# Self-attention row maxima: two key halves in two row halves of the array, one 1024-column reduction

## The reference, cut to what matters

```
q, k, v = (h @ wq), (h @ wk), (h @ wv)            # 1024 x 1024, as 16 heads of 64
sim  = einsum("bhid,bhjd->bhij", q, k) * 64**-0.5 # 1024 x 1024 for each head
attn = softmax(sim)                               # over the keys j
out  = einsum("bhij,bhjd->bhid", attn, v)
```

## Time and profile before

| | |
|---|---|
| median of 3 runs | 2324.59 us (2319.39 to 2327.59) |
| the profiled execution's own time | 2328.06 us |
| its span, first to last instruction | 2326.3 us |
| TensorE busy | 2142.8 us (92%) |
| VectorE busy | 1743.6 us (75%) |
| ScalarE busy | 1476.1 us (63%) |
| GpSimd busy | 1155.2 us (50%) |
| self-attention's maxima on TensorE (L831) | 1024 matmuls, 390.5 us busy |
| their reductions on VectorE (L1411) | 1024, 680.2 us busy |

### The profile page before, as it was taken

One profiled execution on the slowest core, in us unless ns is written; L12 is line 12 of the kernel. 1 busy time (PEld: TensorE's weight loads), 2 busy tenths in 40 slices (PEclk: granted clock), 3 DMA queues, 4 the chain that ended last, 5 costly groups with the idle time before them and its releaser, 6 DMA issues.

```text
span 2326.3 us, 59157 instructions
## 1 busy us (share of the span) xinstructions
PE 2142.8 (92%) x25392; PEld 1434.0 (62%) x25392; DVE 1743.6 (75%) x3148; ACT 1476.1 (63%) x1948; POOL 1155.2 (50%) x730
## 2 busy tenths in 40 slices
PE   4999999999899999989989999998998999999899
PEld 1566666675556666667556666666755666667675
DVE  5888888557588888755768888866576888886664
ACT  2788788345388888823547887773353888786342
POOL 3666665233076766622326766652223667664231
PEclk8999999999999999999999999999999999999999
DMA  3222221000132222001032222100103223210000
GB/s 107 71 73 52 61 62 38 10 31 23 51 105 52 58 74 63 18 10 38 24 83 73 52 75 77 43 27 1 38 23 81 70 61 83 61 36 20 10 11 19
DMA packets 60165, 114.19 MB, mean 49 GB/s; under 512 B 9344, under 2 KB 21632, under 8 KB 59904
## 3 DMA queue, kind: packets, MB, share of 16 engines
q1 hardware_dynamic: 59904, 110.41, 17.5%
HBM read 55.72 MB, written 4.19 MB: 26 GB/s over the span
## 4 chain that ended last, share of the span: by engine, by line
PE 65%; DVE 21%; ACT 9%; issue 3%; DMA 1%; POOL 1%; SPq 0%; POOLq 0%; DVEq 0%; ACTq 0%
PE scores L861 7%; DVE minima L1411 7%; PE scores L854 7%; PE work L831 7%; PE scores L746 6%; PE scores L748 6%; PE scores L747 6%; DVE prob L1426 4%; PE work L746 4%; PE work L747 4%; PE work L748 4%; PE work L883 3%; PE work L879 3%; PE work L881 3%; ACT prob L1214 3%
## 5 line engine op out<-in xcount | busy, mean ns | idle before, releaser
L693 POOL TENSOR_TENSOR prob<-prob 128x1024 f16<-128x1024 f32 x256 | 584.7, 2284 | 556.0 <-ACT prob L1215 545.2
L1411 DVE TENSOR_REDUCE minima<-work 128x1 f32<-128x512 f32 x1024 | 680.2, 684 | 43.0 <-PE work L831 29.4
L1214 ACT ACTIVATE prob<-scores 128x1024 f32<-128x1024 f32 x512 | 525.6, 1026 | 129.2 <-PE scores L861 112.0
L1215 ACT ACTIVATE prob<-scores 128x1024 f16<-128x1024 f32 x512 | 523.3, 1022 | 0.0
L883 PE MATMUL work<-vals,prob 128*128 128x65 f16 x4096 | 429.6, 196 | 0.0
L881 PE MATMUL work<-vals,prob 128*128 128x64 f16 x4096 | 429.4, 193 | 0.0
L879 PE MATMUL work<-vals,prob 128*128 128x65 f16 x4096 | 429.0, 193 | 0.4
L879 PEld LDWEIGHTS work<-vals,prob 128*128 128x128 f16 x4096 | 383.1, 99 | 62.1 <-issue 3.1
L881 PEld LDWEIGHTS work<-vals,prob 128*128 128x128 f16 x4096 | 379.9, 97 | 58.2
L831 PE MATMUL work<-ka,qa 128*128 128x512 f16 x1024 | 390.5, 386 | 24.0 <-DVE minima L1411 18.2
L883 PEld LDWEIGHTS work<-vals,prob 128*128 128x128 f16 x4096 | 380.3, 97 | 0.0
(11 more groups left out here) (160 smaller groups left out, 4179.0 us busy)
## 6 DMA issues: line engine op xcount, KB each, us to landing
qa<-staged_q SPq DMA_DIRECT2D x128, 128.0 KB, 2.3
ka<-staged_k SPq DMA_DIRECT2D x128, 128.0 KB, 2.3
raw_even<-in_pairs SPq DMA_DIRECT2D x32, 384.0 KB, 3.3
raw_odd<-in_pairs SPq DMA_DIRECT2D x32, 384.0 KB, 3.3
raw_odd<-in_pieces SPq DMA_DIRECT2D x20, 512.0 KB, 3.7
raw_even<-in_pieces SPq DMA_DIRECT2D x20, 512.0 KB, 3.6
qb<-staged_q SPq DMA_DIRECT2D x64, 128.0 KB, 2.3
kb<-staged_k SPq DMA_DIRECT2D x64, 128.0 KB, 2.3
```

The source lines that it names most:

```text
L693: pool.tensor_tensor(prob[1][:, slot, :], prob32[:, slot, :], prob[0][:, slot, :], ALU.subtract).then_inc(a.polished, 1)
L1214: act.activation(prob32[:, n % RING, :], source, ACT.Exp)
L1215: act.activation(prob[0][:, n % RING, :], source, ACT.Exp)\
L1411: dve.tensor_reduce(minima[:, t, h:h + 1], out[:, :], AX.X, ALU.max, negate=True)\
```

## The change

Only the upper parts are multiplied for the maxima (q_up·k_up), so a product needs 64 rows. The two key halves of a tile are issued one after the other, the first on the head's own 64 rows (`qa` and `ka`), the second on the other 64 rows, where `qa` already holds the upper query parts and a new buffer `kx` holds the upper key parts of keys 512 to 1023. They write the two halves of one tensor `peaks` of two banks, and one reduction of 1024 columns writes the tile's column of `shift16` itself. `combine` and `shift_combined` go. The step stands whole before the score. There is one `peaks` buffer (`PEAK_RING` 1), which the shift's transpose uses too. `kx` lies in `t32` and is filled by one more DMA for each head (`MOVES` 14 in place of 12).

```diff
-SCORE_RING, PEAK_RING, HIGH_RING = 2, 2, 1
-MOVES = 12
+SCORE_RING, PEAK_RING, HIGH_RING = 2, 1, 1
+MOVES = 14
 def maxima(par, head):
-    tiles = [[Step("max", (t, h), par, head, 0) for h in range(BLKS)] for t in range(TILES)]
+    tiles = [[Step("max", t, par, head, 0)] for t in range(TILES)]
     tiles[0] = first + tiles[0]
-    tiles[-1] = tiles[-1] + [Step("combine", 0, par, head, 0)]
 def self_unit(pair, head):
-        out += [step for step in peaks_of[s] if step.kind == "arrive"] + peaks[:1]
+        out += peaks_of[s]
         out += placed[s]
         out.append(Step("score", s, par, head, 0))
         out += [take(step) for step in placed[s] if step.kind in HIGH]
-        out += peaks[1:] + [step for step in peaks_of[s] if step.kind == "combine"]
 # buffers
-        work = [ps(f"work{i}", BLK) for i in range(4)]
-        self_peaks = [work[0], work[2]]
+        peaks = ps("peaks", 2 * BLK)
+        work = [peaks[:, 0:BLK], ps("work1", BLK), peaks[:, BLK:2 * BLK], ps("work3", BLK)]
+        kx = [t32[:, i, :, :].rearrange("p c n -> p (c n)").bitcast(F16)[:, 0:BLK] for i in range(2)]
 # SP
-                            moves = [(ka_[mine, :], up), (ka_[others, :], low), (kb_[mine, :], up)]
+                            moves = [(ka_[mine, :], up), (ka_[others, :], low), (kb_[mine, :], up),
+                                     (kx[step.par][others, :], up[:, BLK:TOKENS])]
 # TensorE
-                    pe.wait_ge(a.peak_free, pace.n(*PEAK) + 1)
+                    pe.wait_ge(a.peak_free, pace.n(*PEAK) + PEAK_RING)
-                        pe.matmul(out[:, :], qa[par][head][:, t * P:(t + 1) * P],
-                                  ka[par][head][:, h * BLK:(h + 1) * BLK], start=True, stop=True)\
-                            .then_inc(a.peak_full, 1)
+                        mine, others = [slice(r, r + DH) for r in (head * DH, (1 - head) * DH)]
+                        for h, (rows_, keys) in enumerate(((mine, ka[par][head][mine, 0:BLK]),
+                                                           (others, kx[par][others, :]))):
+                            last = pe.matmul(work[2 * h], qa[par][head][rows_, s * P:(s + 1) * P], keys,
+                                             start=True, stop=True)
+                        last.then_inc(a.peak_full, 1)
                     elif step.kind == "shift":
-                        pe.wait_ge(a.shift_combined, pace.n("shift") + 1)
 # VectorE
-                        dve.tensor_reduce(minima[:, t, h:h + 1], out[:, :], AX.X, ALU.max, negate=True)\
+                        dve.tensor_reduce(shift16[:, s:s + 1], peaks[:, :], AX.X, ALU.max, negate=True)\
                            .then_inc(a.peak_free, 1)
-                    elif step.kind == "combine":
-                        dve.wait_ge(a.peak_free, pace.n(*PEAK) + PEAK_RING)
-                        dve.tensor_reduce(shift16[:, :], minima[:, :, :], AX.X, ALU.min)\
-                           .then_inc(a.shift_combined, 1)
```

More of the change, by code:

```diff
@@ L215, in self_unit @@
     for s in range(TILES):
-        peaks = [step for step in peaks_of[s] if step.kind == "max"]
         if s == TILES - 1 and after:
             out.append(Step("shift", 0, *nxt, 0))
-        out += [step for step in peaks_of[s] if step.kind == "arrive"] + peaks[:1]
+        out += peaks_of[s]
         out += placed[s]
@@ L390, in build @@
         prob = [sb(f"prob{i}", [P, 4, TOKENS], F16) for i in range(2)]
-        minima = sb("minima", [P, TILES, 2])
         shift16 = sb("shift16", [P, TILES], F16)
@@ L445, in build @@
         names = ("peak_full peak_free work_full work_high work_free scores_full exp_done refined polished probs_used "
-                 "outs_free inverse_ready head0_ready head1_ready shift_combined row_ready")
+                 "outs_free inverse_ready head0_ready head1_ready row_ready")
         a = collections.namedtuple("Sems", names)(*[sem(f"self_{n}") for n in names.split()])
@@ L766, in next_peak @@
                 def next_peak():
-                    pe.wait_ge(a.peak_free, pace.n(*PEAK) + 1)
-                    return self_peaks[pace.here(*PEAK) % PEAK_RING]
+                    pe.wait_ge(a.peak_free, pace.n(*PEAK) + PEAK_RING)
                 def weight(kind, c, column):
@@ L825, in do @@
                     elif step.kind == "max":
-                        if head == 1 and s == (0, 0):
+                        if head == 1 and s == 0:
                             pe.wait_ge(a.head1_ready, pace.n("arrive", times=8 * MOVES) + CREDIT)
-                        out = next_peak()
-                        t, h = s
-                        pe.matmul(out[:, :], qa[par][head][:, t * P:(t + 1) * P],
-                                  ka[par][head][:, h * BLK:(h + 1) * BLK], start=True, stop=True)\
-                            .then_inc(a.peak_full, 1)
+                        next_peak()
+                        mine, others = [slice(r, r + DH) for r in (head * DH, (1 - head) * DH)]
[4 more added lines that the diff above has]
+                        last.then_inc(a.peak_full, 1)
                     elif step.kind == "shift":
-                        out = next_peak()
-                        pe.wait_ge(a.shift_combined, pace.n("shift") + 1)
-                        pe.transpose(out[0:TILES, 0:P // 2].bitcast(F16), shift16[:, :], ident16[:, :])\
+                        next_peak()
+                        pe.transpose(work[0][0:TILES, 0:P // 2].bitcast(F16), shift16[:, :], ident16[:, :])\
                           .then_inc(a.peak_full, 1)
@@ L1405, in do @@
                     elif step.kind == "max":
[L1406 to L1410, removed]
-                        dve.tensor_reduce(minima[:, t, h:h + 1], out[:, :], AX.X, ALU.max, negate=True)\
+                        next_peak()
+                        dve.tensor_reduce(shift16[:, s:s + 1], peaks[:, :], AX.X, ALU.max, negate=True)\
                            .then_inc(a.peak_free, 1)
-                    elif step.kind == "combine":
-                        dve.wait_ge(a.peak_free, pace.n(*PEAK) + PEAK_RING)
-                        dve.tensor_reduce(shift16[:, :], minima[:, :, :], AX.X, ALU.min)\
-                           .then_inc(a.shift_combined, 1)
                     elif step.kind == "shift":
-                        out = next_peak()
+                        next_peak()
                         dve.wait_ge(a.row_ready, pace.n("shift", times=16) + CREDIT)
-                        dve.tensor_copy(shift_rows[:, :], out[0:TILES, 0:P // 2].bitcast(F16))\
+                        dve.tensor_copy(shift_rows[:, :], work[0][0:TILES, 0:P // 2].bitcast(F16))\
                            .then_inc(a.peak_free, 1)
```

## The result

The changed kernel takes 2356.21 us (median of 4, 2352.65 to 2358.05), the kernel before 2325.03 (4, 2319.39 to 2327.59): 1.0136 times as long, 95% interval 1.0113 to 1.0158. It is slower by 31 us, where 15 were forecast. The sign was right, but by luck: only half of the size was forecast, the term that was to make the kernel slower is not there, and the loss comes mostly from places that the sum had at nothing or too small.

A forecast was written before the change was run, and what follows sets the result against it. TensorE's stream was taken to bound most of a unit, VectorE's order its end. 64 × (0.52 − 0.34) = +11.5 us, and +4 before the units, gave +15 us: 2340 us, 0.6% slower, range 2238 to 2388.

The forecast's parts named there:

- The sign: Whole kernel: slower, by 15 us; chances 0.44 slower, 0.43 faster, 0.13 no change.
- What bounds the kernel: In a unit: TensorE back to back for most of it, VectorE's order deciding at its end.
- TensorE, the cost after: Six pairs of 64-row products a unit: 0.495 us each with 0.235 excess, 2.89 against 2.37, +0.52 us a unit.
- rivals 1 and 2: Rival 1: 64 rows come and go free, 2250 us, chance 0.30; rival 2: products not side by side, about 2406, 0.12.
- VectorE at the unit's end: Chain at the unit's end: reduction and `combine` leave, a wait for the copy enters; −0.34 us a unit, bounds 0 and −0.6.
- Before the units: Tiles standing alone, one buffer: 2.6 us more in the first round, with the later rounds +4 us together.
- DMAs: SP's queue, two more DMAs for each pair of heads: costs nothing; up to 19 us if the cover went.
- Rival 3: Bare steps: one buffer makes TensorE wait 0.3 us in 3 of 8 steps; 58 us, 2398 us, chance 0.10.

The follow-up runs named there:

- the serial rows: The changed kernel with both products of a tile on the head's own 64 rows, one after the other, without the two added DMAs: 2434.54 us.
- The longer queue alone: The kernel before with the change's two more DMAs for each pair of heads, into a buffer that nothing reads: 2336.09 us.
- full rows: The changed kernel with both products of a tile over all 128 rows and without the two added DMAs: 2368.52 us.
- the early split: The changed kernel with GpSimd's split of weights in pair 0 at step 0 of the unit instead of step 3: 2344.31 us.
- The order alone: The kernel before with both products of a tile ahead of the score in steps 0 to 6, two banks and `combine` kept: 2318.22 us.
- three edits: The later fetch, the early split and the later gather together: 2312.94 us in the changed kernel, 2319.31 us in the kernel before.
- the later fetch: The changed kernel with the weight fetch of step 6 moved behind the shift row in SP's queue: 2346.75 us.
- the later gather: The changed kernel with VectorE's gather of step 6 moved from ahead of the shift's copy to behind it: 2337.25 us.
- the order and all three: The kernel before with both products of a tile ahead of the score, plus the three edits: 2307.09 us.

## Why the prediction was right or wrong

- **What bounds the kernel**: right. The two places, TensorE's stream and VectorE's order at the unit's end, are where the steady units moved.
- **TensorE, the cost after**: the step that failed first, mis-sized. The mechanism (side by side, and a drain) was right, and rivals 1 and 2 are refuted by the rows of the pair and by the serial rows. But 0.495 was 0.41: beyond one product it is 0.195 in all, where 0.031 + 0.235 + 0.015 was taken., the eight transposes, were carried over almost whole, and a pair of 64 rows comes in and out for less. 6 × 0.41 − 0.085 = 2.38 against 2.37: the term of +0.52 a unit, 33 us of the sum, is zero; a pair of units takes 45.54, not 45.9. The forecast's sign hung on it, so that the right sign is luck.
- **VectorE at the unit's end**: the wait that turns into a wait for the copy came as told, and the end itself is 0.4 shorter (0.34 forecast). But "out" for the reduction of tile 6 overlooked the take that now stands behind a whole reduction: L746 waits 8.7 us for L1382 (4.1 before). An undisturbed unit is 0.23 longer or 0.26 shorter, about nothing on the mean, where −0.34, or 22 us of the sum, was taken. It is the upper bound that the prediction named for the term. So the two largest terms, +33 and −22 us, were both near nothing: −2.1 us for all undisturbed units.
- **Before the units**: too small. +2.6 was +6.0. The alternation with one buffer is dearer at the lower clock (4.4 in place of 2.6), and the first product comes 2.6 later. Of that, 1.7 us is there at the first query DMA already (33.29 against 31.60). It belongs mostly to this execution: in the four other traces of the changed kernel in which this start is unaltered the DMA is issued at 31.77 to 32.37. The added move ahead of the first pair, 0.64, was left out of the sum.
- **DMAs**: wrong, and the step that failed plainly. "So nothing" rested on one pair in which the shift row left at 170.39 with 0.6 of room. Other pairs had none: six scores waited for the row before the change already. The longer queue alone, with the unit's end as before, makes the odd units 5.5 us longer, against 6.7 in the changed kernel, so that the shorter end adds little. By the medians it is 9 us by moving the fetch, 11 in the kernel before. The prediction's bound, 19, holds it.
- **Rival 3**, one buffer makes TensorE wait: not in the bare steps (2.02 us), as argued, since the divided pair ends early; with full rows it does show.
- **The clock**, which had no place in the sum: where `refine` is late beside GpSimd, TensorE waits, and behind that its clock fell. That is 7.9 us in unit 1, of which the early split gives 5.7 back, and 4.7 in unit 12. The order alone shows both falls with two buffers (unit 1 in three rounds, unit 12 in two), so that the order is enough to bring them. In the trace of before such a `refine` takes 3.54 in unit 12 of round 2; it was not looked for.

The 31 us are thus 38 of delays that three edits take away again, less 6 that the change gains without them. By its own run the later fetch gives 9 us, the early split 12 (6 to 8 in its trace) and the later gather 19; 5 of the sum the kernel before has as well. What decides a fall of the clock stays open. Behind the same wait of 1.53 us unit 12 falls in two rounds of four in the changed kernel and with the early split or the later gather, in three with the later fetch, and in none with all three; with the order and all three, where the waits differ, it falls in two.

## What to carry to other kernels

Splitting the array saved the second product here and paid it back in going in and out, on every pair; whether more products between the two make it pay was not tried. Make a wait on the last buffer short before you take away the second buffer: here it was a wait of 38.8 us for a copy, and moving one gather gave 19 back. A delay of 1 us in VectorE's order cost another 1.5 to 2 us where TensorE's clock fell behind it. And when a queue gets longer, look at the room in all units, not in one.

## What the runs showed of the hardware that was not expected

- An operation on 64 of 128 rows between operations on all 128 costs 0.09 to 0.10 us going in and 0.10 going out, whether one or both halves work.
- A VectorE subtraction of 1024 columns (1.22 us) that starts while GpSimd subtracts or adds ends 1.07 or 1.08 after GpSimd does, 2.30 and 3.95 after its own start; a reduction that reads PSUM isn't held up.
- After waits of 1.43 and 0.54 us close together TensorE ran at a mean granted clock of 0.65 over the next 3.7 us; after 0.43 and 0.54 it stayed at 1.00. A single wait was followed by a fall as well, but not each time: after 1.79 us, with no wait behind it, unit 1 fell to 0.93 in three rounds of four (the order alone); after 1.64 to 1.67 in the kernel before it stayed at 1.00 in all four.
